# Criss-cross attention on one core: the residual added by accumulating transfers, columns written over, one scan chunk in two bounded by ScalarE

## The reference

```python
q = einsum('bchw,oc->bohw', x, Wq) + bq     # 64 channels
k = einsum('bchw,oc->bohw', x, Wk) + bk     # 64 channels
v = einsum('bchw,oc->bohw', x, Wv) + bv     # 512 channels
eH = einsum('bchw,bcpw->bhwp', q, k)        # along the column, own pixel masked out
eW = einsum('bchw,bchp->bhwp', q, k)        # along the row
att = softmax(concatenate([eH, eW], axis=3), axis=3)
out = gamma * (outH + outW) + x             # outH, outW: v weighted by the two halves of att
```

## Time and profile before

| | us |
|---|---|
| runs, median of 3 | 4566.75 |
| profiled execution, device time | 4574.0 |
| its span | 4572.2 |
| prologue, until the first looped batch | 321 |
| the seven looped batches | 3890 |
| last batch | 361 |

### The profile page before, as it was taken

The page is one execution under the profiler, slowest core; times in us unless marked ns, Lnnn a source line. Parts: engine busy times, 40 slices in busy tenths (PEclk is TensorE's granted clock), DMA queues, the critical chain, the costliest instruction groups (busy, mean ns, idle before and its releaser), DMA issues.

```text
span 4572.2 us, 96032 instructions
## 1 busy us (share of the span) xinstructions
PE 3525.7 (77%) x33624; PEld 2418.0 (53%) x33624; DVE 2972.1 (65%) x4282; ACT 1716.7 (38%) x3660; POOL 506.9 (11%) x691
## 2 busy tenths in 40 slices
PE   3986888678876778767788678886787868877676
PEld 2543565445654556545565355563565635655565
DVE  6746775476764866639666386574775747856576
ACT  2434442353423534235242352433433334333431
POOL 0000120001200022000210002100031000300210
PEclk9997798887998789887899878997698986989577
DMA  7967779976889669896698876988769987799489
GB/s 283 299 184 237 245 239 296 290 232 231 271 274 309 211 232 281 264 299 219 217 311 268 272 250 192 338 267 250 261 186 318 292 235 252 204 317 290 148 256 298
DMA packets 753781, 1179.38 MB, mean 258 GB/s; under 512 B 50800, under 2 KB 568432, under 8 KB 744048
## 3 DMA queue, kind: packets, MB, share of 16 engines
q1 hardware_dynamic: 434256, 831.89, 57.7%
q10 hardware_dynamic: 319008, 340.88, 23.1%
HBM read 832.83 MB, written 339.74 MB: 256 GB/s over the span
## 4 chain that ended last, share of the span: by engine, by line
issue 72%; PE 9%; POOL 9%; DVE 4%; DMA 4%; ACT 1%; SPq 1%; POOLq 0%; ACTq 0%; DVEq 0%
POOL qk_lo L455 3%; POOL prob_col L473 3%; POOL prob_row L473 2%; DVE acc L835 2%; PE banks L967 2%; PE banks L969 2%; PE banks L968 2%; DMA v_in<-v_pixel_major 1%; DMA acc<-x 1%; PE banks L1035 1%; DMA out<-acc 1%; PE banks L1037 1%; PE banks L1036 1%; DMA x_first<-x 1%; SPq L361 1%
## 5 line engine op out<-in xcount | busy, mean ns | idle before, releaser
L835 DVE SCALAR_TENSOR_TENSOR acc<-banks,att,acc 128x384 f32<-128x384 f32 x1536 | 1130.0, 797 | 198.9 <-DMA acc<-x 127.2
L967 PE MATMUL banks<-wv_hi,x_hi 128*128 128x512 f16 x2304 | 929.1, 403 | 395.6 <-DVE x_lo L757 394.9
L765 DVE SCALAR_TENSOR_TENSOR v_out<-banks,proj,v_out 128x512 f16<-128x512 f32 x576 | 431.5, 749 | 1134.1 <-ACT v_out L559 1133.5
L968 PE MATMUL banks<-wv_lo,x_hi 128*128 128x512 f16 x2304 | 923.7, 401 | 0.0
L969 PE MATMUL banks<-wv_hi,x_lo 128*128 128x512 f16 x2304 | 919.3, 399 | 0.0
L559 ACT ACTIVATE v_out<-banks,proj 128x512 f16<-128x512 f32 x576 | 390.3, 682 | 859.6 <-PE banks L969 829.2
L1035 PE MATMUL banks<-prob_col,v_in 96*128 96x96 f16 x3072 | 465.5, 214 | 242.1 <-DVE acc L835 236.1
L455 POOL TENSOR_TENSOR qk_lo<-qk_f,qk_hi 128x256 f16<-128x256 f32 x288 | 193.3, 671 | 3567.0 <-ACT qk_hi L567 3559.4
L967 PEld LDWEIGHTS banks<-wv_hi,x_hi 128*128 128x128 f16 x2304 | 235.5, 102 | 663.5 <-issue 456.3
L1035 PE MATMUL banks<-prob_row,v_in 96*128 96x96 f16 x3072 | 456.3, 213 | 101.9 <-DMA v_in<-v_pixel_major 49.8
L1007 PE MATMUL banks<-k_hi,q_both 128*96 128x96 f16 x1536 | 365.1, 295 | 212.4 <-ACT prob_row L606 164.8
(11 more groups left out here) (100 smaller groups left out, 6374.2 us busy)
## 6 DMA issues: line engine op xcount, KB each, us to landing
v_in<-v_pixel_major SPq DMA_DIRECT2D x768, 384.0 KB, 6.0
x_raw<-x ACTq DMA_DIRECT2D x290, 512.0 KB, 7.2
x_next<-x SPq DMA_DIRECT2D x192, 768.0 KB, 4.3
v_pixel_major<-v_out ACTq DMA_DIRECT2D x576, 256.0 KB, 4.0
out<-acc SPq DMA_DIRECT2D x384, 384.0 KB, 10.6
acc<-x SPq DMA_DIRECT2D x192, 384.0 KB, 12.6
acc<-x SPq DMA_DIRECT2D x8, 4608.0 KB, 13.7
acc<-x SPq DMA_DIRECT2D x16, 2304.0 KB, 18.9
```

The costliest lines, as they stand in the source:

```text
L765: nc.vector.scalar_tensor_tensor(out=v_out[tile % V_OUT][:, :, 1, :], in0=bank[tile % 2][:, :].rearrange("p (t c) -> p t c", t=CT), scalar ...
L835: nc.vector.scalar_tensor_tensor(out=a, in0=out_bank[g % OUTS], scalar=att[:, O_FACTOR:O_FACTOR + 1], in1=a, op0=ALU.mult, op1=ALU.add,).t ...
L967: nc.tensor.matmul(dst, s_hi, m_hi, start=(t == 0), stop=False)
L968: nc.tensor.matmul(dst, s_hi, m_lo, start=False, stop=False)
```

## The change

- **Residual.** acc is no longer filled with x. The first writer of a chunk, the column groups, overwrites it with O_FACTOR times PSUM plus the bias gamma times bv: ScalarE does so for `tt` = 0, DVE for `tt` = 1 (`evacuate_column`). Rows are added by DVE as before (`add_row`). Then POOL issues a transfer that adds x to the chunk in SBUF (`add_residual`, `accum_op`, two groups behind), and SP stores the chunk when that has landed, 14 groups behind. `add_bias` and `reload_residual` are gone, and with them the loads L384 to L389. Columns of the second half wait until all chunks of the first are stored.
- **Scan.** Every second chunk is bounded by ScalarE, by its sum of absolute values in place of their maximum (an upper bound as well), into the same table of maxima. A chunk is loaded by two transfers of half the width.
- **q and k.** They are loaded in 48 transfers of 2304 bytes a partition (`QK_PIECES` = 8), and stored with one transfer a block where there were two.
- **Items.** `HEAD` 18 to 20, `STATS` 14 to 6, so that each half of attention has 30 items in place of 27. `TURN` stays 10.
- **Constants.** The mask is -1e30, and one lower bound is 1.0.

```diff
-    HEAD = 18
-    STATS = 14
+    QK_PIECES = 8
+    HEAD = 20
+    STATS = 6
     TURN = 10
-    LATE = 16
-    SETTLE = 3
-    STORE_LAG = 6
+    RES_LAG = 2
+    STORE_LAG = 14
...
             def load_next(batch, scan, c):
-                sp.wait_ge(x_next_seen, scan * SCAN + c + 1)
-                sp.dma_start(
-                    x_next[c % NXT][:, :], x_scan[batch, :, c * SCW:(c + 1) * SCW]
-                ).then_inc(x_next_loaded[c % NXT], 16)
+                sp.wait_ge(x_next_seen[c % NXT], scan * (SCAN // NXT) + c // NXT + 1)
+                for w in range(0, SCW, SCW // 2):
+                    sp.dma_start(
+                        x_next[c % NXT][:, w:w + SCW // 2], x_scan[batch, :, c * SCW + w:c * SCW + w + SCW // 2]
+                    ).then_inc(x_next_loaded[c % NXT], 16)
...
-                for c in range(2):
-                    px = slice(c * HW // 2, (c + 1) * HW // 2)
+                for piece in range(QK_PIECES):
+                    c = piece * 2 // QK_PIECES
+                    px = slice(piece * HW // QK_PIECES, (piece + 1) * HW // QK_PIECES)
...
             def store_chunk(b, g):
-                sp.wait_ge(bias_added, b * (CT * NCH) + tp * (TT * NCH) + (h // 2) * TT + tt + 1)
+                sp.wait_ge(res_added[tt][h // 2], b * (TP * 16) + tp * 16 + 16)
                 sp.dma_start(out_acc[b, tp * TT + tt, :, px], acc[tt][:, px]).then_inc(out_stored[tt][h // 2], 16)
...
-                sp.dma_start(acc[0][:, :], x_acc[b, 0, :, :]).then_inc(acc_loaded[0], 16)
-                sp.dma_start(acc[1][:, 0:HW // 2], x_acc[b, 1, :, 0:HW // 2]).then_inc(acc_loaded[1], 16)
...
+            def add_residual(b, g):
+                tp, o, h, tt = group_at(g)
+                px = slice(h // 2 * CH, (h // 2 + 1) * CH)
+                pool.wait_ge(row_added, b * (GROUPS // 2) + row_number(g) + 1 + ONE0)
+                pool.dma_start(
+                    acc[tt][:, px], x_acc[b, tp * TT + tt, :, px], accum_op=ALU.add
+                ).then_inc(res_added[tt][h // 2], 16)
...
+            def see_next(scan, c):
+                if c == 1:
+                    wait_alone(act, xmax_own_ready, scan + 1)
+                act.wait_ge(x_next_loaded[1], scan * (SCAN // NXT * 32) + (c // NXT + 1) * 32)
+                nc.scalar.activation(
+                    x_next[1][:, :], x_next[1][:, :], ACT.Abs, accum_out=xmax_blk[:, c:c + 1]
+                ).then_inc(x_next_seen[1], 1)
...
-            def add_bias(b, g):
+            def evacuate_column(b, g):
                 tp, o, h, tt = group_at(g)
-                px = slice(h // 2 * CH, (h // 2 + 1) * CH)
-                act.wait_ge(acc_added, b * GROUPS + g + 1 + ADDED0)
+                if h == 0 and tp == 0:
+                    wait_alone(act, s_ready, (b + 1) * PAIRS)
+                if h == 0 and tp > 0:
+                    for c in range(NCH):
+                        wait_alone(act, out_stored[tt][c], b * (TP * 16) + tp * 16 + 16)
+                act.wait_ge(o_mm, b * GROUPS + g + 1 + ONE0)
                 nc.scalar.activation(
-                    acc[tt][:, px], acc[tt][:, px], ACT.Identity, bias=gbv_col[:, tp * TT + tt:tp * TT + tt + 1]
-                ).then_inc(bias_added, 1)
+                    acc_strips[tt][COL][:, h * G:(h + 1) * G, :], out_bank[g % OUTS], ACT.Identity,
+                    scale=att[:, O_FACTOR:O_FACTOR + 1], bias=gbv_col[:, tp * TT + tt:tp * TT + tt + 1],
+                ).then_inc(col_act, 1)
...
+                nc.vector.tensor_scalar(
+                    acc_strips[tt][COL][:, h * G:(h + 1) * G, :], out_bank[g % OUTS], att[:, O_FACTOR:O_FACTOR + 1],
+                    gbv_col[:, tp * TT + tt:tp * TT + tt + 1], ALU.mult, ALU.add,
+                ).then_inc(col_dve, 1)
```

More of the change, by code:

```diff
@@ L146, in criss_cross_attention @@
     qk_f32, _ = place("qk_f32", [P, BLK], F32)
-    qk_hi = [place(f"qk_hi{s}", [P, BLK], F16)[0] for s in range(2)]
-    qk_lo = [place(f"qk_lo{s}", [P, BLK], F16)[0] for s in range(2)]
+    qk_pair = [place(f"qk_pair{s}", [P, 2, BLK], F16)[0] for s in range(2)]
     v_in = [place(f"v_in{u}", [L, G, TT, 2, P], F16)[0] for u in range(VU)]
@@ L204, in criss_cross_attention @@
         x_next_loaded = [sem(f"x_next_loaded{s}") for s in range(NXT)]
-        x_next_seen = sem("x_next_seen")
+        x_next_seen = [sem(f"x_next_seen{s}") for s in range(NXT)]
         xmax_own_ready = sem("xmax_own_ready")
@@ L248, in criss_cross_attention @@
         o_mm = sem("o_mm")
-        acc_loaded = [sem(f"acc_loaded{tt}") for tt in range(TT)]
-        acc_added = sem("acc_added")
-        bias_added = sem("bias_added")
+        col_act = sem("col_act")
+        col_dve = sem("col_dve")
+        row_added = sem("row_added")
+        res_added = [[sem(f"res_added{tt}_{c}") for c in range(NCH)] for tt in range(TT)]
         out_stored = [[sem(f"out_stored{tt}_{c}") for c in range(NCH)] for tt in range(TT)]
-        QK_MM0, V_READY0, QK_READY0, SPLIT0, E0, P0, ADDED0, ONE0 = 2, 2, 2, 2, 2, 2, OUTS, 1
+        QK_MM0, V_READY0, QK_READY0, SPLIT0, E0, P0, ONE0 = 2, 2, 2, 2, 2, 2, 1
         CHAIN = 7
@@ L401, in batch @@
                                 store_chunk(b, last)
[L402 to L409, removed]
             with sp.Fori(0, SCAN // FIRST) as i:
@@ L501, in batch @@
                             normalise(b, g // TT + LA)
+                        if g % HALF >= RES_LAG:
+                            tp, o, h, tt = group_at(g - RES_LAG)
+                            if o == ROW and h % 2:
+                                add_residual(b, g - RES_LAG)
+                        if g % HALF == HALF - 1:
+                            for last in range(g - RES_LAG + 1, g + 1):
+                                add_residual(b, last)
             reduce_xmax(0)
@@ L631, in batch @@
                     exp_pair(b, p)
+                    if items:
+                        for c in scan_at_pair(p):
+                            if c % 2 == 1:
+                                see_next(b + 1, c)
                 for k in range(STATS):
@@ L646, in batch @@
                             high_parts(b, g // TT + AHEAD)
-                        if g % HALF >= SETTLE:
-                            tp, o, h, tt = group_at(g - SETTLE)
-                            if o == ROW and h % 2:
-                                add_bias(b, g - SETTLE)
-                        if g % HALF == HALF - 1:
-                            for last in range(g - SETTLE + 1, g + 1):
-                                if group_at(last)[2] % 2:
-                                    add_bias(b, last)
+                        if o == COL and tt == 0:
+                            evacuate_column(b, g)
                 if items:
@@ L662, in _ @@
                 item(0, i)
+                c, late = divmod(i - 4 - PROLOGUE_LAG, 3)
+                if late == 0 and 0 <= c < SCAN and c % 2 == 1:
+                    see_next(0, c)
             split_hi(1, 0)
@@ L721, in make_scales @@
                 step(1, nc.vector.tensor_scalar(bound[:, 0:1], xmax[:, :], wmax[:, 0:1], wmax[:, 2:3], ALU.mult, ALU.add))
[L722 removed]
+                step(2, nc.vector.tensor_scalar(bound[:, 0:1], bound[:, 0:1], 1.0, None, ALU.max))
                 step(3, nc.vector.tensor_scalar(
@@ L943, in _ @@
                 c, late = divmod(i - 4 - PROLOGUE_LAG, 3)
-                if late == 0 and 0 <= c < SCAN:
+                if late == 0 and 0 <= c < SCAN and c % 2 == 0:
                     see_next(0, c)
```

95 lines of the change are left out of this document (55 added, 40 removed).

## The result

The changed kernel takes 4620.48 us, the median of four runs, against 4568.77 us for the kernel before in the same series: a ratio of 1.0111, 95% interval 1.0095 to 1.0128. It is slower by 1.1%; 4502 us and a gain of 1.4% were forecast. The profiled execution has a span of 4609.9 us.

A forecast was written before the change was run, and what follows sets the result against it. DMA engines bound rows-with-turn and second-rows-to-first-score. Terms summed to -12.6 us a batch, -88 over seven; with the last batch -65 on 4574.0, giving 4509, or 4502 us as median. Range 4350 to 4750.

The forecast's parts named there:

- The accumulating transfer, the weakest number: Transfers adding x to acc: a packet of 3072 bytes takes 170 ns, against 130 plain; a chunk 1.36 us.
- only one leg is doubled: Reason for 170 ns, nearer the lower end of 130 to 260: only one leg doubles, its second read from SBUF.
- The rival of the two reads: DMA-bound stretches: an accumulating packet costs two plain ones, 260 ns, total 4778 us; deciding from 191 ns; chance 0.28.
- q and k: Second rows to next first score: smaller packets of q and k load faster; 5 us a batch taken, between none and 11.
- only reorders them: Same stretch: ScalarE's 28.8 us wait for x blocks shrinks to some 8, but this gains no time, all transfers being the bound.
- First rows, turn, second columns: Attention from first rows through second columns: +9.6 us for rows and turn, -3.4 for second columns, a batch.
- The path at the turn keeps its links: Turn between attention's halves: last add, transfer of x, store, first column, where it was store, then x; no change counted.
- Second rows to first score: From second rows to the next batch's first score: 24 accumulating chunks come in, unhidden; +22.7 us a batch.
- The sums and the first columns: Sums lose 9.4 MB of x and 8 items, -32.6 us; first columns lose PE's waits for DVE, -3.9 us.
- Row scores: Row scores: six of twelve reductions move from DVE to ScalarE; -5.0 us a batch (0 to -10).
- the prologue at 0: Prologue before the looped batches: it runs at the items' pace, so the change costs 0.
- Last batch: Last batch: -15 us in the first columns, +38 us in the rest for the added transfers.

## Why the prediction was wrong, step by step

**The accumulating transfer, the weakest number: mis-sized, 170 ns against 255.** 85 ns are 0.68 us a chunk and 261 us of all engines in 384 chunks; by the 0.84 of the run with plain transfers some 220 us of time (an estimate). This is the step that decides the sign: alone it turns the forecast gain into a loss. Its argument ("only one leg is doubled", and mixed loads and stores at 115 ns) took a rate of many streams for slack in one engine. The rival of the two reads had the price (260 ns), the place (two DMA-bound stretches) and the point from which it decides (191 ns); what it didn't have is the total, 4778, because other terms were mis-sized the other way.

**q and k: mis-sized, 5 us a batch against 13** in HEAD. I had the rate about right (5 against some 7), but "only reorders them" was wrong: the wait for x blocks left PE idle in a stretch that the DMA engines didn't fill (share 0.91 there, 1.00 with pieces). 94 us of the whole where I had 35.

**First rows, turn, second columns: +6.2 forecast, +3.5 measured, for the wrong reasons.** With the price as it is I would have said 0.68 x 24 = 16 more, +22. "The path at the turn keeps its links" was the failed step: before, a reload stands behind a store and the first column waits for both; after, x is in the chunk before the store. In parts (rows, turn, columns) the stretch went from 74.1 + 28.4 + 78.1 us to 92.4 + 29.4 + 62.3: the rows are 18 longer, and the columns 16 shorter where I had 3.4. With plain transfers it is 75.4 + 27.9 + 60.1 = 163.4 us against 180.6, 17 less with the same bytes, all of it in the columns. There DVE had waited 11.8 us for x, and I kept that wait in the sum.

**Second rows to first score: +22.7 forecast, +23.9 measured, by luck.** The price adds 16 to the forecast and q and k take 8 from it, which makes +31; what took the other 7 stays open. The mechanism (no cover for x in the second rows) was right: without any residual transfer the stretch takes 127.3 us, not 162.

**The sums and the first columns: right** (-32.6 against -29.3, -3.9 against -4.4), though ScalarE's column group took 1022 ns instead of 0.7 us. Its cover, an idle ScalarE, held: 45.89 of 76.20 us busy.

**Row scores: wrong in sign.** -5.0 forecast, +6.2 measured. That DVE was busy for 56.56 of 63.8 us didn't make it the bound: ScalarE evacuates for the items too, and what it does in between delays them. A third of the 6.2 is the scan itself, 1.2 at most the shift of the items, and 2.7 go with late landings (by the runs above). I had also put the prologue at 0, where the shared scan costs 7 to 13 us.

**Last batch: +23 forecast, +40.2 measured.** The transfer's price is the larger part (35 us less without the addition). What I missed besides is its opening, until its first score, 23.0 us before and 34.8 after. The 48 issues of q and k aren't the cause: in the kernel before with 48 pieces it takes 20.9 us, in the changed kernel with 12 transfers 37.1. It is the chain from the seventh batch: the first transfer of q is issued 4.1 us after the batch opens before, and 17.1 us after it in the changed kernel, for SP's last stores still wait for residual transfers. SP's waits between 4200 and 4232 us, before and after:

```profile
SPq L361 <- ACT acc L619: 7.9, 6, 3.8
SPq L369 <- DMA acc<-x: 17.7, 4, 10.6
```

The prediction had named this chain for the looped batches, where items stand beside it, and not for the last one, where none do. The first columns gave back 27 us instead of 15, and the rest lost 57 instead of 38.

**The account of the whole**: q and k in pieces -94 us on the kernel before (112 on the changed one); the scan on ScalarE +18 on the one kernel, +30 on the other; accumulating in place of plain transfers +321; what is left to overwriting, the missing first fill and the moved items is 52 + 94 - 321 - (18 to 30), near -200 us, a remainder that no run has alone, and as uncertain as these parts are different on the two kernels.

## What to carry to other kernels

Where the DMA engines' share is 1, price a transfer by the engine's time per packet, and count an accumulating one as two plain ones of its size. An addition in the transfer saves an instruction on an engine that has room and pays in the resource that is full; load plainly into a small buffer and add there. A store that waits for such a transfer passes the delay on to whatever stands behind it on its queue. When a large change comes out near zero, run its small parts alone: one constant held 94 us here, and it would have been kept without the rest.

## What was not expected of the hardware

- 64 partitions by 9216 bytes in a packet load at 14.9 bytes a ns an engine and hold back ACT's queue (240 GB/s in all, one wait of 28.8 us for x); the same bytes in rows of 2304 leave 324 GB/s.
- POOL's queue joins rows of plain loads: 3072 bytes a partition went in packets of 6144. Accumulating transfers went in packets of 3072 (2816 of them in 22 chunks).
- An accumulating transfer takes POOL 977 ns to issue, a plain one of the same shape 551.
- A strided column write of 384 elements takes 945 ns on DVE and 1022 ns on ScalarE, where the contiguous row addition with one operand more takes 609 ns.
